# Token mixer: the add of the two partial products of the data moves from GpSimd to VectorE

## The chip, the cores and the metric

One Trainium2 chip, one core. The metric is the device time of the whole program in microseconds, the median of several runs. The cores' engines are named TensorE (PE in the profile), VectorE (DVE), ScalarE (ACT), GpSimd (POOL) and SyncE (SP), which here issues the DMAs.

## The reference

The model makes 64 sequences of 128 image rows and 77 text rows, each of 1024 values, and passes them through a selective scan and a quantized dense layer. Only the first part, the token mixer, is touched. For each of the 128 heads h it builds a kernel from 64 complex modes n and applies it to 64 channels of data c:

```
Wc = W * (exp(dtLambda) - 1) * reciprocal((exp(dtLambda * L) - 1) * Lambda)   # complex, W is the input x
P  = dtLambda[..., None] * pos - P_max[..., None]
K  = einsum('chn,hnl->chl', Wc, exp(P)).real                                   # 64 x 128 x 1024
h  = concatenate([K, txt], axis=1)                                             # then scan, dense layer
```

All of it is f32. The data x is complex, so the product of the data with the complex factor of each mode is a sum of two real products: that sum is the add which the change moves.

## The kernel before, in words

`build` runs its parts one behind the other: `constants`, `token_mixer`, `dense_weights`, `scan_pass` and a general path that is normally empty. The end of a part is a point at which all engines meet. `token_mixer` has 16 steps (G = 0 to 15) of 8 heads each. The first four steps are written out, the other twelve run in a hardware loop of two steps a turn. Partitions hold 64 modes, real parts in the first 64 and imaginary parts in the last 64. The 1024 positions of a head are split: the table (`mag`) has 256 positions, and the data (`gw`) is multiplied with four shifted factors (NQ = 4), so that one matmul of `gw` with `mag` gives all four quarters.

In a step G the engines do this, each in its own order; semaphores tie them:

- VectorE (lines 397 to 422): the angles of 8 heads (line 401, eight instructions, reading one SBUF tensor), their rounding (405) and the subtraction (407), which raises `reduced`. Then, from PSUM, the data times the real factor into `gw` (two instructions of four heads) and times the imaginary factor into `cross` (two more, both line 416, the latter raise `crossed`). Then `evacuate(G - 1)`: the copies of PSUM bank 3 to SBUF (line 395) for heads 3 and 7 of the step before.
- ScalarE (284 to 295): eight Exps for the magnitudes into `mag` (288), the Sin of the angles into `osc` (293) after `reduced`, then the copies of banks 0 to 2 of the step before (282): heads 0, 1, 2, then 4, 5, 6.
- GpSimd (301 to 313): for each side of four heads `mag` times `osc` (line 309, raises `table`), and `gw` plus `cross` (line 312, raises `scaled`).
- TensorE (`step`, lines 443 to 460): head 0 of the step before, the 64 small transposes of this step's data into PSUM (455, raises `x_turned`), and then heads 1 to 7 of the step before (438). A head needs `scaled`, `table` and an empty bank: four banks serve eight heads, so head 4 waits until bank 0 has been copied out, and head 7 until bank 3 has been.
- SyncE: the data of the step after next (line 245, `load`) and the store of the 2 MB of results (252, `store`), two transfers each.

`gw`, `mag`, `res` and the loaded data have two buffers, taken in turns by steps; `cross`, `ang`, `near` and `osc` have one. Nothing else plans the order: it is as written in these step functions.

Of the kernel before, what the change touches and what calls it, by code (L numbers as in the profile page):

```python
# [16 lines left out]
ALU = mybir.AluOpType  # L17
# [22 lines left out]
HG = 8  # L40
# [8 lines left out]
def wait(engine, sem, value):  # L49

    if isinstance(value, int) and value <= 0:
        return
    engine.wait_ge(sem, value)
# [115 lines left out]
def token_mixer(nc, t, dram, mixed):  # L169
# [5 lines left out]
    with ExitStack() as ctx:  # L175
# [24 lines left out]
        cross = sb("t_cross", [P, HG, NQ, BATCH])  # L200
        gw = sb("t_gw", [P, 2, HG, NQ, BATCH])
# [11 lines left out]
        x_turned, crossed, scaled = sem("t_x_turned"), sem("t_crossed"), sem("t_scaled")  # L213
# [7 lines left out]
        def loop(engine, step, tail=None):  # L221

            for G in range(4):
                step(G, G % 2, G == 0)
            with engine.Fori(2, NG // 2) as i:
                step(i * 2, 0, False)
                step(i * 2 + 1, 1, False)
            if tail:
                tail(NG - 1, (NG - 1) % 2)
# [5 lines left out]
        @block.sync  # L235
        def _(sp):
            sp.dma_start(ldt[:, :], dram["log_dt"].rearrange("h r -> (h r)").unsqueeze(0).broadcast_to([P, 2 * HEADS])).then_inc(loaded, 16)
            for k in range(2):
                sp.dma_start(lam[64 * k:64 * k + 64, :], dram["Lambda"]).then_inc(loaded, 16)

            def load(G, half):

                wait(sp, x_turned, G - 1)
                for side in range(2):
                    sp.dma_start(xg[64 * side:64 * side + 64, half, :].rearrange("c (h m) -> c h m", h=HG // 2),
                                 x[:, bass.ds(G * HG + HG // 2 * side, HG // 2), :]).then_inc(x_in[half], 16)

            def store(G, half):
                for b in range(4):
                    wait(sp, empty[b], 2 * G + 2)  # L250
                for a in range(2):
                    sp.dma_start(mixed[:, bass.ds(G * HG, HG), :].rearrange("c h (b a l) -> a c h b l", b=2, a=2)[a],
                                 res[64 * a:64 * a + 64, half, :, :, :]).then_inc(out_done[half], 16)

            load(0, 0)
            load(1, 1)
            with sp.Fori(1, NG // 2) as i:
                load(i * 2, 0)
                store(i * 2 - 2, 0)
                load(i * 2 + 1, 1)  # L260
                store(i * 2 - 1, 1)
            store(NG - 2, 0)
            store(NG - 1, 1)
            for half in range(2):
                sp.wait_ge(out_done[half], 32 * (NG // 2))
# [33 lines left out]
        @block.gpsimd  # L299
        def _(pool):  # L300
            def step(G, half, first):

                for side in range(2):
                    s = slice(side * HG // 2 * QL, (side + 1) * HG // 2 * QL)
                    heads = slice(side * HG // 2, (side + 1) * HG // 2)
                    if side == 0:
                        pool.wait_ge(sine_done, G + 1)
                        pool.wait_ge(mag_done, G + 1)
                    nc.gpsimd.tensor_tensor(mag[:, half, s], mag[:, half, s], osc[:, s], ALU.mult).then_inc(table, 1)  # L309
                    flat = lambda z: z.rearrange("p h a c -> p (h a c)")  # L310
                    pool.wait_ge(crossed, 2 * G + side + 1)
                    nc.gpsimd.tensor_tensor(flat(gw[:, half, heads, :, :]), flat(gw[:, half, heads, :, :]), flat(cross[:, heads, :, :]),
                                            ALU.add).then_inc(scaled, 1)
            loop(pool, step)

        @block.vector
        def _(dve):
            n = [0]
            L = lambda ins: link(dve, dve_step, n, ins)
            V = nc.vector  # L320
# [67 lines left out]
            def evacuate(G, half):  # L388

                wait(dve, out_done[half], out_count(G, half))  # L390
                for h in range(HG):
                    b = h % 4
                    if b in DVE_BANKS:
                        dve.wait_ge(full[b], 2 * G + h // 4 + 1)
                        V.tensor_copy(res[:, half, h, :, :].rearrange("p b l -> p (b l)"), kb[b][:, :]).then_inc(empty[b], 1)

            def step(G, half, first):

                wait(dve, sine_done, G)
                for h in range(HG):  # L400
                    last = V.tensor_scalar(ang[:, h * QL:(h + 1) * QL], pos[:, :], turns[:, bass.ds(G * HG + h, 1)],
                                           role[:, 1:2], ALU.mult, ALU.add)
                last.then_inc(turned, 1)
                dve.wait_ge(turned, G + 1)
                V.tensor_scalar(near[:, :], ang[:, :], ROUND, ROUND, ALU.add, ALU.subtract).then_inc(rounded, 1)
                dve.wait_ge(rounded, G + 1)
                V.tensor_tensor(ang[:, :], ang[:, :], near[:, :], ALU.subtract).then_inc(reduced, 1)

                dve.wait_ge(x_turned, G + 1)
                wait(dve, full[3], 2 * (G - 1))  # L410
                wait(dve, scaled, 2 * G)
                for order, g, target in ((0, gre, gw[:, half, :, :, :]), (1, gim, cross[:, :, :, :])):
                    for side in range(2):
                        heads = slice(HG // 2 * side, HG // 2 * side + HG // 2)
                        data = turned_x[:, side, 256 * order:256 * order + 256].rearrange("p (h c) -> p h c", c=BATCH)
                        last = V.tensor_tensor(
                            target[:, heads, :, :], data.unsqueeze(2).broadcast_to([P, HG // 2, NQ, BATCH]),
                            g[:, bass.ds(G * HG + HG // 2 * side, HG // 2), :].unsqueeze(3).broadcast_to([P, HG // 2, NQ, BATCH]), ALU.mult)
                        if order == 1:
                            last.then_inc(crossed, 1)  # L420
                if not first:
                    evacuate(G - 1, 1 - half)

            loop(dve, step, evacuate)

        @block.tensor
# [1112 lines left out]
```

## Time and profile before

| | us |
|---|---|
| median of 3 runs | 6348.16 |
| lowest and highest | 6346.99, 6351.74 |
| the profiled execution, its own time | 6355.26 |
| its span, first to last instruction | 6353.5 |
| token mixer steps 4 to 14 in it | 188.85 |
| everything after the token mixer | 6008.83 |

The span is what the profile's offsets count from. "Busy" is time in which the engine executes; an interval in brackets at the end of a timeline row is the idle time before it and what ended it. Instructions on one engine may overlap a little at their ends. TensorE's granted clock is given as a share of its full speed: 1.00 is 2.4 GHz and 0.50 is 1.2 GHz.

### The profile page before, as it was taken

The numbers are of one execution on the slowest core, as the hardware profiler recorded it, in microseconds if no ns is written. First come the engines' busy times: TensorE is split into PE (matmuls) and PEld (weight loads), VectorE is DVE, ScalarE is ACT, GpSimd is POOL, SyncE is SP. The second block draws the span as 40 slices with busy tenths as digits, with TensorE's granted clock in tenths as the row PEclk, the third lists the DMA queues.
The fourth block names the chain that finished last, engine by engine and source line by source line (L and its number), as shares of the span: only waits on it lengthen the run. The fifth ranks groups of instructions, "written<-read, shape, count | busy, mean of one in ns | idle before, by whom it ended". The sixth has DMA issues, their size and how long they took to land. (4 is left out here: it accounts for less than half of the span.)

```text
span 6353.5 us, 110648 instructions
## 1 busy us (share of the span) xinstructions
PE 5868.1 (92%) x34115; PEld 5413.4 (85%) x34131; DVE 5699.0 (90%) x4609; ACT 5187.5 (82%) x13015; POOL 5718.5 (90%) x3724
## 2 busy tenths in 40 slices
PE   4667899999999999999999999999999999999998
PEld 3433799999999999999999999999899999999997
DVE  7833999999999999999999999999999999999996
ACT  4646788888888888888888888888888888888885
POOL 3501999999999999999999999999999999999995
PEclk8788999999999999999999999999999999999999
DMA  3510122122211222122221222212222122212220
GB/s 80 139 34 32 70 86 76 62 78 86 86 71 64 81 86 81 65 76 81 86 81 60 79 83 86 76 64 77 86 86 70 65 81 86 81 60 79 83 81 33
DMA packets 113795, 478.62 MB, mean 75 GB/s; under 512 B 13345, under 2 KB 50353, under 8 KB 105074
## 3 DMA queue, kind: packets, MB, share of 16 engines
q1 hardware_dynamic: 113266, 471.63, 21.4%
q8 instruction: 325, 5.32, 0.4%
q14 instruction: 204, 1.67, 0.1%
HBM read 328.35 MB, written 143.24 MB: 74 GB/s over the span
## 5 line engine op out<-in xcount | busy, mean ns | idle before, releaser
L1083 POOL TENSOR_TENSOR s_ring<-s_bc,s_u_t 128x820 f32<-128x820 f32 x2048 | 3626.2, 1790 | 3.5 <-DMA s_bc<-rows_bc 3.5
L989 ACT ACTIVATE s_decay<-s_dt_t,a_neg 128x205 f32<-128x205 f32 x8192 | 3047.2, 420 | 428.4 <-DVE s_ring L1154 360.6
L886 PE MATMUL s_y_ps<-s_ring,ident 128*128 128x205 f32 x16384 | 3166.0, 343 | 138.6 <-POOL s_ring L1089 69.0
L886 PEld LDWEIGHTS s_y_ps<-s_ring,ident 128*128 128x128 f32 x16384 | 2888.5, 193 | 227.1 <-POOL s_ring L1089 133.6
L1148 DVE TENSOR_TENSOR_SCAN s_decay<-s_decay,s_ring 128x820 f32<-128x820 f32 x1216 | 2265.4, 1863 | 221.9 <-ACT s_decay L989 219.3
L1089 POOL TENSOR_TENSOR s_ring<-s_ring,s_bc 128x820 f32<-128x820 f32 x832 | 1607.5, 1932 | 52.1 <-DVE s_ring L1148 52.0
L1148 DVE TENSOR_TENSOR_SCAN s_ring<-s_decay,s_ring 128x820 f32<-128x820 f32 x832 | 1543.6, 1855 | 45.2 <-ACT s_decay L989 44.6
L919 PE MATMUL s_xch<-s_x_t,w_low 128*128 128x205 f32 x8192 | 1522.5, 338 | 0.6 <-ACT s_x_t L1029 0.2
L919 PEld LDWEIGHTS s_xch<-s_x_t,w_low 128*128 128x128 f32 x8192 | 1424.1, 190 | 32.8 <-issue 30.5
L1154 DVE TENSOR_TENSOR s_ring<-s_decay,s_bc 128x820 f32<-128x820 f32 x1216 | 1230.1, 1012 | 41.8
L1029 ACT ACTIVATE s_x_t<-s_xch 128x512 f32<-128x512 f32 (+1 forms) x512 | 245.8, 505 | 92.8 <-PE s_xch L910 90.9
L880 PE MATMUL s_y_ps<-s_x_t,s_d_diag 128*128 128x205 f32 x1024 | 278.6, 354 | 34.9 <-ACT s_x_t L1024 34.9
L1024 ACT ACTIVATE s_x_t<-s_y_ps 128x205 f32<-128x205 f32 x512 | 171.1, 334 | 168.1 <-PE s_y_ps L886 167.3
L1043 ACT ACTIVATE s_y_t<-s_xch,y_bias 128x205 f32<-128x205 f32 x512 | 214.2, 418 | 104.4 <-PE s_xch L919 104.4
L1104 POOL TENSOR_TENSOR s_u_t<-s_dt_t,s_x_t 128x410 f32<-128x410 f32 x256 | 272.3, 1064 | 18.5 <-DVE s_dt_t L1176 18.5
L438 PE MATMUL t_kb<-t_mag,t_gw 128*128 128x256 f32 x512 | 154.7, 469 | 135.7 <-ACT t_res L282 99.3
L438 PEld LDWEIGHTS t_kb<-t_mag,t_gw 128*128 128x128 f32 x512 | 120.4, 241 | 164.5 <-issue 141.4
L951 PE MATMUL s_p_ps<-s_xp,dtw_t 33*128 33x205 f32 x1024 | 247.4, 362 | 7.6 <-DVE s_dt_t L1176 7.1
L880 PEld LDWEIGHTS s_y_ps<-s_x_t,s_d_diag 128*128 128x128 f32 x1024 | 169.2, 189 | 75.4 <-ACT s_x_t L1024 57.2
L309 POOL TENSOR_TENSOR t_mag<-t_mag,t_osc 128x1024 f32<-128x1024 f32 x32 | 75.4, 2355 | 173.6 <-ACT t_osc L293 173.6
L1127 POOL MEMSET s_large<- 128x4 f32 x1 | 0.1, 102 | 247.5 <-POOLq L496 247.5
L951 PEld LDWEIGHTS s_p_ps<-s_xp,dtw_t 33*128 33x128 f32 x1024 | 165.7, 187 | 66.3 <-issue 56.7
(161 smaller groups left out, 4608.9 us busy)
## 6 DMA issues: line engine op xcount, KB each, us to landing
s_bc<-rows_bc SPq DMA_DIRECT2D x64, 3280.0 KB, 11.2
mixed<-t_res SPq DMA_DIRECT2D x32, 1024.0 KB, 10.3
s_x_in<-mixed SPq DMA_DIRECT2D x64, 512.0 KB
s_h<-mixed SPq DMA_DIRECT2D x64, 512.0 KB
before<-s_h SPq DMA_DIRECT2D x64, 512.0 KB
out<-s_h SPq DMA_DIRECT2D x64, 512.0 KB
s_x_in<-in_txt SPq DMA_DIRECT2D x64, 308.0 KB
s_h<-in_txt SPq DMA_DIRECT2D x64, 308.0 KB
```

The lines of the kernel that those rows point to most:

```text
L438: last = nc.tensor.matmul(kb[b][:, QL * k:QL * k + QL], gw[:, half, h, 2 * k:2 * k + 2, :], mag[:, half, h * QL:(h + 1) * QL], start=True, ...
L880: nc.tensor.matmul(y_ps, d_diag[:, j, :], x_t[:, par, j, :], start=True, stop=False)
L886: last = nc.tensor.matmul(y_ps, ident[:, :], ring[:, c % RING, n * LEN:(n + 1) * LEN], start=False, stop=(c % 4 == 3 and n == CN - 1))
L919: last = nc.tensor.matmul(bank[:, 0:LEN], t["w_low"][:, i, P * o:P * o + P], x2_t[:, i, :], start=(i == 0), stop=(i == ND - 1))
L951: last = nc.tensor.matmul(p_ps[:, LEN * k:LEN * k + LEN], t["dtw_t"][:, P * j:P * j + P], xp[0:RANK + 1, :], start=True, stop=True)
L989: last = A.activation(decay[s % 2][:, n * LEN:(n + 1) * LEN], dt_t[:, par, j, :], ACT.Exp, scale=t["a_neg"][:, j, n0 + n:n0 + n + 1])
L1029: A.activation(target[:, 4 * side:4 * side + 4, cols(k)], bank[:, 0:4 * w].rearrange("p (j l) -> p j l", j=4), ACT.Copy).then_inc(empty, 1)
L1083: nc.gpsimd.tensor_tensor(ring[:, s % RING, :].rearrange("p (n l) -> p n l", n=CN), bc[:, par, n0:n0 + CN, :], u_t[:, j, :].unsqueeze(1).b ...
L1089: nc.gpsimd.tensor_tensor(ring[:, c % RING, :], ring[:, c % RING, :], bc[:, par, n0:n0 + CN, :].rearrange("p n l -> p (n l)"), ALU.mult).t ...
L1104: nc.gpsimd.tensor_tensor(u_t[:, 2 * r:2 * r + 2, :], dt_t[:, par, 2 * r:2 * r + 2, :], x_t[:, par, 2 * r:2 * r + 2, :], ALU.mult).then_in ...
L1148: V.tensor_tensor_scan(out=decay[s % 2] if s in ON_DVE else ring[:, s % RING, :], data0=decay[s % 2], data1=ring[:, s % RING, :], initial= ...
L1154: V.tensor_tensor(ring[:, s % RING, :], decay[s % 2], bc[:, par, n0:n0 + CN, :].rearrange("p n l -> p (n l)"), ALU.mult).then_inc(dve_hc, 1)
```

## The change

GpSimd no longer adds: its step holds only the two multiplies of line 309, and their waits. VectorE does the two adds of four heads each, behind its four products and ahead of its copies of bank 3. Each add waits for `crossed` of its side, a semaphore that VectorE itself raised, and raises `scaled` as before. VectorE's own wait on `scaled` before it overwrites `cross` is gone, since the same engine now reads it earlier in its order. TensorE's waits are unchanged.

```diff
--- before.py
+++ after.py
@@ -302,15 +302,10 @@
 
                 for side in range(2):
                     s = slice(side * HG // 2 * QL, (side + 1) * HG // 2 * QL)
-                    heads = slice(side * HG // 2, (side + 1) * HG // 2)
                     if side == 0:
                         pool.wait_ge(sine_done, G + 1)
                         pool.wait_ge(mag_done, G + 1)
                     nc.gpsimd.tensor_tensor(mag[:, half, s], mag[:, half, s], osc[:, s], ALU.mult).then_inc(table, 1)
-                    flat = lambda z: z.rearrange("p h a c -> p (h a c)")
-                    pool.wait_ge(crossed, 2 * G + side + 1)
-                    nc.gpsimd.tensor_tensor(flat(gw[:, half, heads, :, :]), flat(gw[:, half, heads, :, :]), flat(cross[:, heads, :, :]),
-                                            ALU.add).then_inc(scaled, 1)
             loop(pool, step)
 
         @block.vector
@@ -408,7 +403,6 @@
 
                 dve.wait_ge(x_turned, G + 1)
                 wait(dve, full[3], 2 * (G - 1))
-                wait(dve, scaled, 2 * G)
                 for order, g, target in ((0, gre, gw[:, half, :, :, :]), (1, gim, cross[:, :, :, :])):
                     for side in range(2):
                         heads = slice(HG // 2 * side, HG // 2 * side + HG // 2)
@@ -418,6 +412,12 @@
                             g[:, bass.ds(G * HG + HG // 2 * side, HG // 2), :].unsqueeze(3).broadcast_to([P, HG // 2, NQ, BATCH]), ALU.mult)
                         if order == 1:
                             last.then_inc(crossed, 1)
+                flat = lambda z: z.rearrange("p h a c -> p (h a c)")
+                for side in range(2):
+                    heads = slice(HG // 2 * side, HG // 2 * side + HG // 2)
+                    dve.wait_ge(crossed, 2 * G + side + 1)
+                    V.tensor_tensor(flat(gw[:, half, heads, :, :]), flat(gw[:, half, heads, :, :]), flat(cross[:, heads, :, :]),
+                                    ALU.add).then_inc(scaled, 1)
                 if not first:
                     evacuate(G - 1, 1 - half)
 
```

## Rows read from the trace of the kernel before

**Rows 1.** The page: busy time of each engine, share of the span, and count.

```profile
PE 5868.1 (92%) x34115; PEld 5413.4 (85%) x34131; DVE 5699.0 (90%) x4609; ACT 5187.5 (82%) x13015; POOL 5718.5 (90%) x3724
```

**Rows 2.** Table by stage: start:end, length, busy per engine, granted clock, DMA share, GB/s.

```profile
117.02:305.87 188.85, 117.88 (x1057) 94.33 (x1056) 150.34 (x177) 121.33 (x188) 101.26 (x44) 0.80 0.58 138
...
344.67:6353.50 6008.83, 5691.74 (x32562) 5272.59 (x32578) 5449.87 (x4280) 5005.08 (x12737) 5567.73 (x3649) 0.98 0.20 73
```

**Rows 3.** Timeline of step 14: start, us, engine, line, operation, out<-in, count, idle before.

```profile
288.80 4.72 DVE L401 TENSOR_SCALAR t_ang<-t_pos,t_turns,t_role 128x256 f32<-128x256 f32 x8
...
288.99 2.45 POOL L312 TENSOR_TENSOR t_gw<-t_gw,t_cross 128x1024 f32<-128x1024 f32 x1
...
290.07 2.86 PE L438 MATMUL t_kb<-t_mag,t_gw 128*128 128x256 f32 x12
...
294.82 2.29 DVE L407 TENSOR_TENSOR t_ang<-t_ang,t_near 128x2048 f32<-128x2048 f32 x1
297.03 2.35 DVE L416 TENSOR_TENSOR t_gw<-t_turned_x,t_gre 128x1024 f32<-128x1024 f32 x2
297.14 1.91 ACT L293 ACTIVATE t_osc<-t_ang 128x2048 f32<-128x2048 f32 x1 [2.98 <-DVE t_ang L407]
298.96 1.55 ACT L282 ACTIVATE t_res<-t_kb 128x512 f32<-128x512 f32 x3
299.13 2.35 POOL L309 TENSOR_TENSOR t_mag<-t_mag,t_osc 128x1024 f32<-128x1024 f32 x1 [7.70 <-ACT t_osc L293]
299.29 2.35 DVE L416 TENSOR_TENSOR t_cross<-t_turned_x,t_gim 128x1024 f32<-128x1024 f32 x2
...
299.68 6.40 PE L438 MATMUL t_kb<-t_mag,t_gw 128*128 128x256 f32 x20 [6.76 <-ACT t_res L282]
...
301.56 0.68 DVE L395 COPY t_res<-t_kb 128x512 f32<-128x512 f32 x1
301.76 0.60 ACT L282 ACTIVATE t_res<-t_kb 128x512 f32<-128x512 f32 x1 [1.25 <-PE t_kb L438]
303.47 0.60 ACT L282 ACTIVATE t_res<-t_kb 128x512 f32<-128x512 f32 x1 [1.11 <-PE t_kb L438]
...
304.40 0.60 ACT L282 ACTIVATE t_res<-t_kb 128x512 f32<-128x512 f32 x1 [0.33 <-PE t_kb L438]
305.26 0.69 DVE L395 COPY t_res<-t_kb 128x512 f32<-128x512 f32 x1 [3.02 <-PE t_kb L438]
...
305.87 4.72 DVE L401 TENSOR_SCALAR t_ang<-t_pos,t_turns,t_role 128x256 f32<-128x256 f32 x8
...
306.06 2.44 POOL L312 TENSOR_TENSOR t_gw<-t_gw,t_cross 128x1024 f32<-128x1024 f32 x1
```

**Rows 4.** Timeline of steps 0 to 3: the angles (line 401), one table load.

```profile
45.51 2.67 DVE L401 TENSOR_SCALAR t_ang<-t_pos,t_turns,t_role 128x256 f32<-128x256 f32 x8
...
56.22 8.72 DVE L401 TENSOR_SCALAR t_ang<-t_pos,t_turns,t_role 128x256 f32<-128x256 f32 x8
...
79.60 3.99 DVE L401 TENSOR_SCALAR t_ang<-t_pos,t_turns,t_role 128x256 f32<-128x256 f32 x8
...
87.25 1.28 ACT L293 ACT_TABLE_LOAD   x1 [4.11 <-DVE t_ang L407]
...
97.47 4.77 DVE L401 TENSOR_SCALAR t_ang<-t_pos,t_turns,t_role 128x256 f32<-128x256 f32 x8
```

**Rows 5.** Table by stage, one slice of step 14, with its columns' names.

```profile
core 0: us, PE busy (x) PEld busy (x) DVE busy (x) ACT busy (x) POOL busy (x), PEclk, DMA share, GB/s
297.00:303.00 6.00, 3.32 (x8) 2.72 (x9) 5.24 (x6) 3.97 (x5) 3.87 (x2) 0.50 0.61 152
```

**Rows 6.** One line in the scan pass: durations in ns, minimum, median and maximum.

```profile
L1154 DVE TENSOR_TENSOR s_ring<-s_decay,s_bc x1216: 1010/1012/1015, 619.0 to 6284.6; 128x820 f32<-128x820 f32 x174
```

**Rows 7.** Timeline of the scan pass: that line beside a GpSimd multiply.

```profile
3013.75 1.93 POOL L1089 TENSOR_TENSOR s_ring<-s_ring,s_bc 128x820 f32<-128x820 f32 x1
...
3014.63 1.01 DVE L1154 TENSOR_TENSOR s_ring<-s_decay,s_bc 128x820 f32<-128x820 f32 x1
```

## The prediction

> **What bounds the kernel now.** I read the page's line of engines first: all five are busy for 82 to 92% of the span [rows 1], so an average says nothing about a change that touches the token mixer alone. The second view is the table by stage: the eleven mixer steps 4 to 14 take 188.85 us, and the 6008.83 us after the mixer hold no changed instruction [rows 2]. In the eleven steps VectorE is busy 150.34 us, GpSimd 101.26 us, TensorE 117.88 us: 80, 54 and 62%. No engine is full, so it is a chain that sets the step, and the third view, the timeline of one step, shows it.
>
> A step begins where VectorE starts its eight angle instructions (line 401). Step 14 runs from 288.80 to 305.87, 17.07 us [rows 3]. Alone the eight take 2.67 us; beside GpSimd they take 3.99, 4.77 and 8.72 us [rows 4], and 4.72 in step 14. GpSimd's last add of the step before ends at 288.99 + 2.45 = 291.44, and the angle work ends at 293.52, 2.08 later: about six of its eight instructions (0.33 each) run only once GpSimd is done. From there: rounding and subtraction end at 297.11 (3.59), ScalarE's Sin at 299.05 (1.94), GpSimd starts at 299.13 its two multiplies and two adds, and the last add ends at 308.50 (9.45, the gap included). 2.08 + 3.59 + 1.94 + 9.45 = 17.06: this loop is the step of 17.07. GpSimd's four instructions bound the mixer, though GpSimd is busy only 54%, because line 401 cannot run beside them. VectorE's and TensorE's other work hangs on the same loop with slack.
>
> **What goes.** Two GpSimd adds in each of 16 steps. GpSimd then has two multiplies, which start where Sin ends: offset 299.13 - 288.80 = 10.33 in today's step. In the new step everything from line 405 on is earlier by 4.72 - 2.67 = 2.05, so they start at 8.28 and end 2 x 2.35 later, at 12.98. The next line 401 starts well after that (below), so it pays 2.67 again. The wait on `scaled` that VectorE loses never was the late one.
>
> **What comes.** Two VectorE adds of 128x1024, both inputs in SBUF. The nearest rows are line 416, same size, one input in PSUM: the two pairs start 2.26 apart, 1.13 each [rows 3]; and line 407, both inputs in SBUF, 2048 elements in 2.29, half of which is 1.15. Bounds for the pair are 2.2 and, if each keeps its own whole duration with nothing overlapped, 2.45. I take 2.27, since the waits on `crossed` are already met when the adds come up (the first half was counted 1.1 us earlier). Behind the adds on VectorE stands the copy of bank 3 (line 395), and for that TensorE's head 7 waits.
>
> **The new step, offsets from its start.** Line 401 ends at 2.67. Line 407 ends at 297.11 - 288.80 - 2.05 = 6.26. Line 416's last ends at 299.29 + 2.35 - 288.80 - 2.05 = 10.79; the overlap of 0.08 seen between neighbours puts the adds at 10.71 to 12.98. Then comes the copy of bank 3, 0.68, to 13.66. TensorE starts about 0.12 after an emptied bank (298.96 + 0.60 to 299.68), so head 7 starts at 13.78. A head started at 299.68 was followed by its copy at 301.76: 2.08, with a pitch of 303.47 - 301.76 = 1.71 at 1.2 GHz; the pitch at 2.4 GHz is 305.26 - 304.40 = 0.86, so start to copy is 0.86 + 0.37 = 1.23 there. At full clock the second copy starts at 15.01, and the next step 0.61 behind it (305.87 - 305.26): 15.62.
>
> Is head 7 at full clock? Head 4 starts when ScalarE has emptied bank 0, at 299.68 - 288.80 - 2.05 = 8.83. TensorE's earlier work ends at 4.13 (290.07 + 2.86 is 4.13 after 288.80), so it idles 4.7 us instead of 6.8. In step 14 the granted clock was 0.50 from 297 to 303 [rows 5], so it had fallen within 4.1 us of TensorE's stop at 292.93, and it came back not before 3.3 us of new work; head 6's copy follows head 5's by 0.93, almost the fast pitch, so not much later than that. With a similar answer head 7 begins between 13.78 and 13.96 (8.83 + 3 x 1.71, three slow heads), just as the clock is back or somewhat before. That makes 15.6 to 16.1 for the step; I take 15.8.
>
> ScalarE does not come in between: in front of Sin it waited for line 407 (2.98 us in step 14), which comes only 2.05 earlier, so its table and Exps still fit [rows 3]. The transfers move with a share of 0.58 of 17.17 us, 10 us a step [rows 2], below 15.8.
>
> **The sum.** Steps 4 to 14: 188.85 - 11 x 15.8 = 15.1. Step 0 to 1: today line 401 of step 1 starts at 56.22 and ends at 64.94; it will start 2.27 later, at 58.49, and last 2.67: 61.16, saving 3.8. Steps 2 and 3: line 401 goes from 3.99 and 4.77 to 2.67, 1.3 + 2.1 = 3.4 [rows 4]; there ScalarE loads the Sin table, 1.28, only after its wait (the loop's steps load it ahead), so all of TensorE's later heads are 1.3 us later, head 7 is not held by the copy, and the whole saving passes. Step 15: as one more steady step, 17.17 - 15.8 = 1.4; behind it the two last stores (10 us each, one behind the other) follow the same shift. 15.1 + 3.8 + 3.4 + 1.4 = 23.7. The profiled execution ran 6355.26 (span 6353.5); 23.7 less is 6331.6. The median of the runs shown is 6348.16, 7.1 below the profiled one, so the prediction is 6348.16 - 23.7 = 6324.5. A measurement tells no more than about 0.2%, 12.7 us, from no change; the threshold for faster is 6335.5.
>
> **A rule that speaks against it.** In the scan pass VectorE's line 1154 reads two SBUF tensors, as the new adds do. All 1216 of them last 1010 to 1015 ns [rows 6]. The one at 3014.63 lies wholly inside a GpSimd multiply from 3013.75 to 3015.68 that reads two SBUF tensors itself [rows 7]. So neither waited for the other.
>
> The Trainium skill, SBUF — State Buffer, section Who interferes with whom, says that a VectorE instruction with two SBUF inputs contends with a GpSimd instruction that reads SBUF, and that the loser blocks fully. The row differs from it for this pair of shapes; by the rule the step would be that of the lock rival below. For line 401 (one SBUF input, the two-port mode) the same section's lock agrees with [rows 4].
>
> **Rivals.**
> (a) *The lock.* The adds reach VectorE at 10.71, while the second multiply runs (10.6 to 12.98). If they wait for it they run from 12.98 to 15.25, the copy ends at 15.93, head 7 starts at 16.05, its copy at 17.28, and the step is 17.89: 11 x 17.89 is 7.9 more than today. Steps 2 and 3, with the table's 1.3 in front, take 19.2 each, 1.0 more than the 37.42 of today (79.60 to 117.02); step 15 loses 0.7; of step 0's 3.8 the 2.2 of waiting goes off, leaving 1.6 saved. The total is 8 us slower, 6356; with head 7 slow, 0.85 more in each of eleven steps, 6365. It decides as soon as the pair of adds costs about 1.6 us more than 2.27 in each of fifteen steps; below that something is still gained. Against it: [rows 6, 7].
> (b) *TensorE stays slow.* If heads 4 to 7 all run at 1.2 GHz, head 7's copy starts at 8.83 + 4 x 1.71 + 0.37 = 16.04, the step is 16.65, and the savings are 5.7 + 3.8 + 3.4 + 0.5 = 13.4: 6334.8. For it: the clock returned only after 3.3 us of work or more in [rows 5], and head 7 starts 5.0 after head 4, close to that; a later return in some steps costs part of it.
> (c) *Nothing arrives at the end.* The gain is real in the mixer and lost behind it, since 6008.83 us follow whose time differs between executions by several us: 6348. Nothing in the profile waits for a fixed time, so I find no cause.
> On the good side: if the clock never falls (idle 4.7 us), the step is 15.62 (17.0 in all eleven), step 1 could be bound by 58.49 + 15.6 = 74.1 instead of 79.60 - 3.8 = 75.8 (1.7 more): 27.4, 6320.8.
>
> **Chances.** Forecast 0.74, (b) 0.12, (c) 0.07, (a) 0.05, something unseen 0.02. The range 6314 to 6339 takes in the full-clock case and (b), each widened by the 4 us of the runs' spread. (a) and (c) lie outside. Faster: the forecast and most of (b), 0.84; same: the rest of (b), (c) and half of (a), 0.13; slower 0.03.
>
> **What would show it.** In the new trace the GpSimd line of the mixer holds 32 multiplies and no add; line 401's eight take 2.67 in every step; the two adds take 2.27 as a pair beside the second multiply (4.5 would be the lock); VectorE's wait in front of the second bank-3 copy falls from 3.0 to about 1.3; TensorE waits for the bank-3 copy ahead of head 7, a wait that today's timeline does not have; steps are 15.6 to 16.1 apart; the stage behind the mixer keeps its 6008.8. Steps of 16.6 with a clock share of 0.5 throughout heads 4 to 7 would be (b). A step near 17, or adds over 3 us, makes the prediction wrong.

## The result: slightly slower, by the exclusion of VectorE's adds and GpSimd's multiplies

The changed kernel took 6359.69 us (median of 20 runs, 6353.53 to 6364.02), the kernel before 6350.65 (20 runs, 6346.3 to 6355.37). The ratio is 1.0014, interval 1.0008 to 1.0021: some 9 us slower. I had forecast 6324.5, with a range of 6314 to 6339. A change of 0.14% is less than the 0.2% that I had set as the threshold, so it is "same" in the terms of the forecast, to which I had given 0.13 (and 0.03 to slower). It is clear of the runs' noise all the same, since the interval lies above 1. The profiled execution of the changed kernel took 6361.02 us, its span is 6359.2.

**Where the time went.** Table by stage of the changed kernel: steps 4 to 14, step 15 with the stores, and all that follows (columns as in [rows 2]).

```profile
117.65:313.91 196.26, 128.96 (x1057) 98.25 (x1056) 179.33 (x200) 121.37 (x188) 51.30 (x22) 0.79 0.56 132
313.91:353.62 39.71, 19.90 (x127) 15.61 (x125) 17.76 (x21) 14.07 (x23) 4.67 (x2) 0.76 0.67 158
353.62:6359.20 6005.58, 5691.16 (x32578) 5269.17 (x32578) 5448.73 (x4280) 5005.72 (x12737) 5567.71 (x3649) 0.98 0.20 73
```

The eleven steps took 196.26 us instead of 188.85 ([rows 2]), 7.4 more: 17.84 a step, not 15.8. Step 4 begins at 117.65, 0.6 later than before, and step 15 with the stores gives 0.9 more (39.71 against 344.67 - 305.87 = 38.80). The next part starts 8.95 us later; what follows it took 3.25 us less in this one execution. GpSimd's busy time fell from 101.26 to 51.30 us, VectorE's rose from 150.34 to 179.33. Line 401 took 48.49 us in these steps before and takes 29.34 now, 19.1 less. VectorE's busy time rose by 29.0 all the same, so the 22 adds account for 29.0 + 19.1 = 48.1, which is 2.2 each and not the forecast's 1.13. Their own busy time in the trace is 49.0.

**One step.** Timeline of the changed kernel's step 14; line 401 is now 396, 407 is 402, 416 is 410, 395 is 390, 309 is 308, and the new adds are line 419 ([rows 3] answers).

```profile
296.32 2.67 DVE L396 TENSOR_SCALAR t_ang<-t_pos,t_turns,t_role 128x256 f32<-128x256 f32 x8
...
300.28 2.29 DVE L402 TENSOR_TENSOR t_ang<-t_ang,t_near 128x2048 f32<-128x2048 f32 x1
...
304.59 4.67 POOL L308 TENSOR_TENSOR t_mag<-t_mag,t_osc 128x1024 f32<-128x1024 f32 x2 [12.92 <-ACT t_osc L293]
304.75 2.34 DVE L410 TENSOR_TENSOR t_cross<-t_turned_x,t_gim 128x1024 f32<-128x1024 f32 x2
...
305.15 5.10 PE L438 MATMUL t_kb<-t_mag,t_gw 128*128 128x256 f32 x12 [4.71 <-ACT t_res L282]
307.02 4.46 DVE L419 TENSOR_TENSOR t_gw<-t_gw,t_cross 128x1024 f32<-128x1024 f32 x2
...
311.40 0.68 DVE L390 COPY t_res<-t_kb 128x512 f32<-128x512 f32 x1
...
312.13 2.80 PE L438 MATMUL t_kb<-t_mag,t_gw 128*128 128x256 f32 x8 [1.88 <-DVE t_res L390]
313.30 0.69 DVE L390 COPY t_res<-t_kb 128x512 f32<-128x512 f32 x1 [1.22 <-PE t_kb L438]
```

Up to 307.02 the forecast holds to 0.1 us. Line 396 takes 2.67; line 402 ends at offset 6.25 (forecast 6.26); GpSimd starts at 8.27 (8.28); head 4 at 8.83 (8.83); the adds come up at 10.70 (10.71). Then the pair takes 4.46 instead of 2.27. GpSimd's second multiply runs from 306.9 to 304.59 + 4.67 = 309.26, the adds end at 311.48, which is 2.22 after it: neither add executed while the multiply did. The wait is not shown as idle time in front of line 419. It lies inside the duration of the first add (3.32 us; the second takes 1.21), and in the busy share. Everything behind pays: the copy of bank 3 at 311.40, head 7 from 312.13 (TensorE idle for 1.88 us, "DVE t_res L390"), the second copy at 313.30, and the next step at 313.91, 17.59 long.

The lines of the two instructions over the whole trace (columns as in [rows 6]):

```profile
L419 DVE TENSOR_TENSOR t_gw<-t_gw,t_cross x32: 1209/2830/3365, 56.1 to 327.9; 128x1024 f32<-128x1024 f32 x32
```

```profile
L308 POOL TENSOR_TENSOR t_mag<-t_mag,t_osc x32: 2346/2357/3332, 53.7 to 324.5; 128x1024 f32<-128x1024 f32 x32
```

The three figures are minimum, median and maximum. An add takes 1209 ns at best. The median of 2830 is the duration of no add: it lies between two groups. In step 0 and in steps 4 to 15 the first add of a step takes 3.31 to 3.33 us and the second 1.21; in steps 1 to 3 they take 2.35 and 3.36. The products of line 410 (416 before) on the same shape, with one input in PSUM, take 1.2 in the same steps. GpSimd's multiply is 2346 at best and 3332 at most, so it is blocked as well. That happens in steps 1 to 3, where Sin ends late and the first add arrives during the first multiply. Timeline of step 1:

```profile
70.14 5.64 POOL L308 TENSOR_TENSOR t_mag<-t_mag,t_osc 128x1024 f32<-128x1024 f32 x2 [11.75 <-ACT t_osc L293]
...
71.22 5.64 DVE L419 TENSOR_TENSOR t_gw<-t_gw,t_cross 128x1024 f32<-128x1024 f32 x2
```

Both pairs last 5.64. The order that fits is multiply, add, multiply, add, each waiting for the one in flight: 2.35 + about 1 + 2.35 + 1.1, counted from the first multiply to the end of the last add (76.86 - 70.14 = 6.72). In step 14 the adds arrived 0.1 us after the second multiply had begun and waited for that one alone.

Four of the eleven steps were 18.0 to 18.5 long, the other seven 17.6 or 17.65. In the four, the granted clock from head 7's start to its copy was 0.69, 0.50, 0.68 and 0.50; in step 14 it was 0.94. Before that TensorE had stood idle behind the blocked adds, 2.57 us in step 8, which follows, and 1.88 in step 14. Timeline, then the table by stage of that head:

```profile
203.57 0.68 DVE L390 COPY t_res<-t_kb 128x512 f32<-128x512 f32 x1
...
204.30 3.49 PE L438 MATMUL t_kb<-t_mag,t_gw 128*128 128x256 f32 x8 [2.57 <-DVE t_res L390]
206.41 0.69 DVE L390 COPY t_res<-t_kb 128x512 f32<-128x512 f32 x1 [2.17 <-PE t_kb L438]
```

```profile
204.30:206.30 2.00, 2.00 (x5) 1.64 (x6) 0.00 (x0) 0.00 (x0) 0.00 (x0) 0.50 0.00 0
```

Head 7's start to its copy is 206.41 - 204.30 = 2.11, where it is 313.30 - 312.13 = 1.17 in step 14: 0.94 more in step 8, where the granted clock is 1.2 GHz at that place. That is the 0.95 by which step 8 (18.54) is longer than step 14.

### The profile page after: what moved, and what is told of

It reads as the page before. It is cut to its first block and busy times, and to the rows that moved or that the text cites. A ratio compares the mean times of both kernels' runs of the same rounds, so it can differ in the third digit from the quotient of the medians.

```text
span 6359.2 us, 110645 instructions
## 1 busy us (share of the span) xinstructions
PE 5882.3 (92%) x34131; PEld 5415.0 (85%) x34131; DVE 5740.7 (90%) x4641; ACT 5188.2 (82%) x13015; POOL 5647.1 (89%) x3692
## 5 line engine op out<-in xcount | busy, mean ns | idle before, releaser
L919 PEld LDWEIGHTS s_xch<-s_x_t,w_low 128*128 128x128 f32 x8192 | 1427.9, 190 | 33.3 <-issue 30.5
```

What stands on the lines that cost most here:

```text
L919: last = nc.tensor.matmul(bank[:, 0:LEN], t["w_low"][:, i, P * o:P * o + P], x2_t[:, i, :], start=(i == 0), stop=(i == ND - 1))
```

## The experiments

The theory after the result: a VectorE instruction with two SBUF inputs and a GpSimd instruction that reads SBUF exclude each other, and in this order the blocked adds hold up head 7's bank. Rivals: the adds are slow for what they are; VectorE's total time sets the step wherever they stand; any GpSimd work excludes them. The steps below are means over steps 4 to 14, from the starts of the angle instructions in each trace. The medians are of 20 runs for the changed kernel and of 4 to 7 for each experiment, against 9 to 20 of the kernel before on the same chip. Each experiment is an edit of the changed kernel.

| kernel | median us | before, same chip | ratio, interval | step |
|---|---|---|---|---|
| before | | 6350.65 | | 17.17 |
| changed | 6359.69 | 6350.65 | 1.0014, 1.0008 to 1.0021 | 17.84 |
| e1_psum_cross | 6329.19 | 6349.69 | 0.9970, 0.9958 to 0.9981 | 15.88 |
| e2_copy_first | 6323.76 | 6349.69 | 0.9966, 0.9952 to 0.9979 | 15.78 |
| e3_no_mult | 6320.52 | 6349.69 | 0.9956, 0.9941 to 0.9971 | 15.57 |
| e4_no_adds | 6320.60 | 6349.69 | 0.9955, 0.9939 to 0.9970 | 15.29 |
| e5_memset | 6322.51 | 6350.68 | 0.9955, 0.9940 to 0.9971 | 15.66 |
| e6_psum_copy_first | 6320.22 | 6350.68 | 0.9953, 0.9939 to 0.9967 | 15.29 |

**e1_psum_cross: the imaginary product in PSUM.**

```diff
-        cross = sb("t_cross", [P, HG, NQ, BATCH])
+        cross_ps = ctx.enter_context(nc.psum_tensor("t_cross_ps", [P, HG // 2 * NQ * BATCH], F32))
...
+                product(0, 0)
+                product(1, 0).then_inc(crossed, 1)
+                product(0, 1)
+                add(0)
+                dve.wait_ge(scaled, 2 * G + 1)
+                product(1, 1).then_inc(crossed, 1)
...
+                add(1)
```

> The imaginary product of the data goes to PSUM (two banks, used by one side after the other) instead of SBUF, so that each VectorE add has one SBUF and one PSUM input; VectorE's order in a step is real 0, imaginary 0, real 1, add 0, imaginary 1, add 1, and one more wait on its own semaphore stands between. GpSimd's multiplies are unchanged. Theory (a VectorE add with two SBUF inputs and a GpSimd multiply that reads SBUF exclude each other): each add takes 1.2 to 1.35 us beside the second multiply, the step falls from 17.6 to 15.7-16.1 us, total 22 to 26 us below the kernel before, about 6327 where the kernel before is 6350.6. Rival (the adds are slow for what they are, in place and 1024 long, and would be so with GpSimd idle or with PSUM): the pair stays near 4.5 us, step 17.6, total 6360.

Timeline of one step:

```profile
244.03 4.67 POOL L308 TENSOR_TENSOR t_mag<-t_mag,t_osc 128x1024 f32<-128x1024 f32 x2 [11.16 <-ACT t_osc L293]
...
245.32 1.21 DVE L419 TENSOR_TENSOR t_gw<-t_gw,t_cross_ps 128x1024 f32<-128x1024 f32 x1
246.65 1.23 DVE L411 TENSOR_TENSOR t_cross_ps<-t_turned_x,t_gim 128x1024 f32<-128x1024 f32 x1
...
247.92 1.22 DVE L419 TENSOR_TENSOR t_gw<-t_gw,t_cross_ps 128x1024 f32<-128x1024 f32 x1
...
249.06 0.68 DVE L390 COPY t_res<-t_kb 128x512 f32<-128x512 f32 x1
...
251.21 0.69 DVE L390 COPY t_res<-t_kb 128x512 f32<-128x512 f32 x1 [1.47 <-PE t_kb L445]
```

and the adds of the whole mixer:

```profile
L419 DVE TENSOR_TENSOR t_gw<-t_gw,t_cross_ps x32: 1210/1216/1223, 55.2 to 295.6; 128x1024 f32<-128x1024 f32 x32
```

GpSimd's pair of multiplies runs from 244.03 to 248.70. The first add (245.32 to 246.53) lies wholly inside it, the second (247.92 to 249.14) for most of its length, and all 32 take 1210 to 1223 ns. Their order differs a little from the changed kernel's, but both still meet the multiplies; what differs is the memory of one input. That the order alone does not free them is shown by e2, which moves the adds and leaves both inputs in SBUF. So the excess came from the second input's being in SBUF. The steps are 15.8 to 16.1 long, 15.88 in the mean, as expected. The kernel is 0.30% faster than the one before, by 20.5 us, a little less than the 22 to 26 expected.

**e2_copy_first: the adds behind the first copy of bank 3.**

```diff
+                def adds():
+                    for side in range(2):
...
+                if first:
+                    adds()
+                else:
+                    evacuate(G - 1, 1 - half, adds)
```

`evacuate` runs `adds` after the copy of head 3.

> The changed kernel, with the two adds behind the first copy of bank 3 (head 3) instead of ahead of it; both inputs stay in SBUF. Theory (exclusion, and the price is paid because head 7's bank stands behind the blocked adds): the add pair still takes over 4 us of VectorE's time or ends when the second multiply ends plus 2.2, but TensorE no longer waits for the copy of bank 3; adds end at offset 15.2, head 7 is ready at 15.2 to 15.5, step 15.9-16.1, total 6328 to 6334 with the kernel before at 6350.6. Rival (VectorE's total time in a step sets it, wherever the adds stand): step 17.6, total 6360.

Timeline of one step:

```profile
245.91 4.67 POOL L308 TENSOR_TENSOR t_mag<-t_mag,t_osc 128x1024 f32<-128x1024 f32 x2 [11.01 <-ACT t_osc L293]
...
248.33 0.68 DVE L390 COPY t_res<-t_kb 128x512 f32<-128x512 f32 x1
...
248.93 3.86 DVE L423 TENSOR_TENSOR t_gw<-t_gw,t_cross 128x1024 f32<-128x1024 f32 x2
...
252.72 0.68 DVE L390 COPY t_res<-t_kb 128x512 f32<-128x512 f32 x1
```

The exclusion is still there: the pair takes 3.86, and ends at 252.79, 2.21 after the multiplies (245.91 + 4.67 = 250.58). But bank 3 was emptied at 249.01, ahead of it, and head 7 was ready when the adds ended: line 390 follows at once, with no wait. The step is 15.68 here and 15.78 in the mean, 2.1 below the changed kernel's mean. Step and total (6323.76) came out below the 15.9 to 16.1 and 6328 to 6334 expected. The rival that VectorE's total sets the step fails. The price was not the blocked 2.2 us as such, but head 7 standing behind them.

**e3_no_mult and e5_memset: what of GpSimd's work excludes.** In e3 a multiply of one element stands for each table multiply; in e5, behind one such multiply, GpSimd writes 128x2048 zeros twice, into a tile of its own. Both leave the oscillation out of the table.

```diff
-                    nc.gpsimd.tensor_tensor(mag[:, half, s], mag[:, half, s], osc[:, s], ALU.mult).then_inc(table, 1)
+                    nc.gpsimd.tensor_tensor(scratch[:, side:side + 1], t["ident"][:, 0:1], t["ident"][:, 1:2], ALU.mult).then_inc(table, 1)
```

```diff
+                    if side == 0:
+                        nc.gpsimd.tensor_tensor(scratch[:, 0:1], t["ident"][:, 0:1], t["ident"][:, 1:2], ALU.mult)
+                    nc.gpsimd.memset(filler[:, side, :], 0.0).then_inc(table, 1)
```

> The changed kernel without GpSimd's two table multiplies (a 1-element multiply holds the semaphore), so the output of the mixer lacks the oscillation. Theory (exclusion): with GpSimd idle each add takes 1.13 to 1.22 us and the pair 2.3; the step is 15.6-16.1, total 6324 to 6331. Rival (adds slow by themselves): pair 4.5, step 17.6, total 6360.

> The changed kernel with GpSimd's two multiplies replaced by two memsets of 128x2048 into a tile of their own: GpSimd is busy at the same place but reads nothing from SBUF (the mixer's output lacks the oscillation). If what excludes the adds is GpSimd's reading, the adds take 1.13 to 1.22 us each even beside a memset, the step is 15.5 and the total that of the kernel without multiplies, 6320. If any GpSimd instruction excludes them, an add that meets a memset lasts until its end plus 1.1, and the step is longer by what is left of the memset, up to 2 us, total up to 6350.

The adds of e3 in the whole mixer, with both inputs in SBUF:

```profile
L420 DVE TENSOR_TENSOR t_gw<-t_gw,t_cross x32: 1215/1217/1220, 56.2 to 291.9; 128x1024 f32<-128x1024 f32 x32
```

The memsets and the adds of e5, one step and then the whole mixer:

```profile
240.88 3.55 POOL L312 MEMSET t_filler<- 128x2048 f32 x2
...
243.17 2.35 DVE L423 TENSOR_TENSOR t_gw<-t_gw,t_cross 128x1024 f32<-128x1024 f32 x2
```

```profile
L423 DVE TENSOR_TENSOR t_gw<-t_gw,t_cross x32: 1215/1218/1222, 56.3 to 290.8; 128x1024 f32<-128x1024 f32 x32
```

With GpSimd idle the same two-SBUF adds take 1.22 us, so they are not slow by themselves. In e5 GpSimd writes from 240.88 to 244.43 and the adds are up from 243.17: the first lies wholly inside the second memset, as it does in every step, and it takes 1.22 us as well. So GpSimd's activity alone does not exclude them; the instruction that does so reads SBUF. A memset also differs from a multiply in kind, and no experiment varies the kind alone; that the reading is what matters fits these runs, but they do not single it out. The total of e3 came out below the 6324 to 6331 expected, and that of e5 at 6322.51 for 6320.

**e4_no_adds: how much VectorE's own time weighs.** The two adds are left out, so the imaginary part of the data is missing. TensorE then waits for the products:

```diff
-                        pe.wait_ge(scaled, 2 * G + h // 4 + 1)
+                        pe.wait_ge(crossed, 2 * G + h // 4 + 1)
```

> The changed kernel without the two adds (TensorE waits for the products instead), so the imaginary part of the data is left out. Theory (the mixer's next limit is head 7 behind TensorE's slow clock, not VectorE's time): step 15.2-15.9, total 6322 to 6330, within 4 us of the kernel without GpSimd's multiplies. Rival (each us of VectorE counts fully): step 2.2 to 4.4 below the step with adds, 13.2 to 13.6 us, total below 6300.

It came out at 6320.60, equal to e3 with all the adds, and 1.4 below the range expected. VectorE waits for head 7 for 2.8 or 3.9 us in each step there:

```profile
215.16 0.69 DVE L390 COPY t_res<-t_kb 128x512 f32<-128x512 f32 x1 [2.80 <-PE t_kb L432]
...
231.08 0.69 DVE L390 COPY t_res<-t_kb 128x512 f32<-128x512 f32 x1 [3.93 <-PE t_kb L432]
```

Its step is 0.28 us shorter than e3's in these traces (15.29 against 15.57), for some 2.3 us less of VectorE's time. So that time counts for a small part at most, and the rival that asked for a step of 13.2 to 13.6 fails. The run also repeated the other exclusion once: line 396 of step 1 took 4.66 us beside the multiplies that remained.

**e6_psum_copy_first: both remedies.** As e1, with the copy of bank 3 between the first add and the second imaginary product.

> Both remedies together: the imaginary product goes to PSUM, and the first copy of bank 3 stands between add 0 and the second imaginary product. Without exclusion and with head 7 released early (copy done at offset 11.5), TensorE's four heads from offset 8.8 set the end: step 15.0 to 15.9, total 6317 to 6326, like the kernel without adds (6320). If the early copy alone already gives all there is (the adds hidden in the shadow of TensorE), it is within 4 us of the kernel with the copy first (6323.8); if PSUM saves what the blocked adds still cost there, it is lower.

The table by stage of two neighbouring steps, and TensorE's heads from 4 on in each:

```profile
216.14:232.06 15.92, 11.22 (x98) 8.93 (x96) 14.29 (x20) 11.03 (x18) 4.66 (x2) 0.79 0.62 148
232.06:246.86 14.80, 10.09 (x97) 8.15 (x96) 14.29 (x20) 11.03 (x18) 4.67 (x2) 0.88 0.67 159
```

```profile
224.97 7.30 PE L451 MATMUL t_kb<-t_mag,t_gw 128*128 128x256 f32 x20 [4.70 <-ACT t_res L282]
...
240.89 6.18 PE L451 MATMUL t_kb<-t_mag,t_gw 128*128 128x256 f32 x20 [4.71 <-ACT t_res L282]
```

This is as fast as the kernel without the adds, and the fastest here that computes everything: 0.47% below the kernel before. By the medians it is not told apart from e2 (their intervals overlap); in the traces its step is 0.49 us shorter in the mean. Its steps alternate between 15.9 and 14.8 us. In both TensorE is idle for 4.7 us; the step is short where the granted clock is 0.88 on average and the heads take 6.18 in place of 7.30 us.

## Why the prediction was wrong

- **What bounds the kernel before: right.** Without GpSimd's adds line 401 takes 2.67 us in every step, in the changed kernel and in all six experiments but for one place, and where nothing new stood in the way the step fell to 15.3 to 15.9. The loop through GpSimd was the bound.
- **"What comes", the pair of adds at 2.27 us: this step failed.** It was 4.46, and 5.64 in three steps: the sum held a time for two adds that run freely, and nothing for their wait behind the multiply. The bounds I gave, 2.2 and 2.45, did not hold it. The failure came from the section on the rule, where I wrote of line 1154 that it "reads two SBUF tensors, as the new adds do". It doesn't. The kernel declares one of its inputs in PSUM (line 730):

```
decay = [ctx.enter_context(nc.psum_tensor(f"s_decay{i}", [P, 1024], F32))[:, EDGE:EDGE + CW] for i in range(2)]
```

  A row of the trace names tiles, not the memory they are in, and I read the name `s_decay` as an SBUF tile. So [rows 6, 7] show what e1 shows, that a VectorE instruction with one PSUM input runs beside GpSimd at full speed, and were no evidence on the case at hand. Nor were the nearest rows, 416 (one input in PSUM) and 407 (two in SBUF, but GpSimd idle beside it). With the true bound the range would have reached to rival (a). The Trainium skill, SBUF — State Buffer, section Who interferes with whom, says that a VectorE instruction with two SBUF inputs contends with a GpSimd instruction that reads SBUF, and not with one that only writes it. That is rival (a), and the runs agree: adds of up to 3.37 us beside the multiplies, 1.22 beside the memsets (e5).
- **Rival (a) at 0.05 was what happened**, nearly in its numbers: adds ending at 15.16 of the step (forecast 15.25), head 7 at 15.81 (16.05), step 17.59 with head 7 fast (17.89), line 401 of step 1 done at 63.18 and not 64.94, a gain of 1.8 (1.6). The total was 6356 to 6365; 6350.65 x 1.0014 is 6359.7. Its addition of 0.85 for a slow head 7 was seen in four steps of eleven, as 0.95 in two and 0.4 in two. What it lacked is that the multiplies are blocked too: with pairs of 5.64 in steps 1 to 3, step 4 began 0.6 later than before, where the rival had it 0.6 earlier (1.6 saved, 1.0 lost).
- **The sum apart from that: right.** e1, which does what I thought the change did, has a step of 15.88 (forecast 15.8, range 15.6 to 16.1), and is 20.5 us below the kernel before (forecast 23.7). In its trace steps 4 to 14 take 174.66 us, a saving of 14.2 (forecast 15.1), and steps 0 to 3 take 63.19 in place of 71.51, a saving of 8.3 (forecast 3.8 + 3.4 = 7.2).
- **The low-clock rival (b)** asked for heads at 1.2 GHz through the step's end. With the exclusion gone (e1) no step was over 16.1. In the e1 step shown, the granted clock was 0.50 from 244.58 to 249.06 and 0.81 over head 7 (1.42 us from its start to its copy, where the forecast had 1.23 at full clock and 2.08 at 1.2 GHz), so head 7 was mostly back at full clock, as forecast; in e4 and e6 every second step shows the difference, 1.1 us.
- **Rival (c), a gain that is lost behind the mixer: refuted by the experiments.** In the traces the last copy of bank 3 ends 23.4 us earlier than in the kernel before in e1, 23.0 in e2, 26.8 in e3, 29.9 in e4, 28.6 in e5 and 29.5 in e6; the medians are 20.5, 25.9, 29.2, 29.1, 28.2 and 30.5 lower. What the mixer gains arrives at the end, to within some 3 us.
- **The wait on `scaled`, the transfers, ScalarE's place:** as forecast, no wait on them stands in the rows above.

## What to carry to other kernels

Before moving work from GpSimd to VectorE, look up for both the memory of every input, in the declarations and not by the tile's name: here a VectorE add with two SBUF inputs did not run beside a GpSimd multiply that reads SBUF, while one with an input in PSUM did. If the collision can't be avoided, put whatever another engine waits for ahead of the instruction that will be blocked; here that order alone turned 0.14% slower into 0.34% faster. A blocked instruction shows as a long one, not as a wait, so compare each duration in a trace with the shortest of the same shape.

## What the runs showed of the hardware that I had not expected

The exclusion works both ways and by single instructions: in steps 1 to 3 multiplies of 2.35 us and adds of 1.2 us took turns, and both pairs lasted 5.64 us. A GpSimd memset beside the same adds cost neither anything: the 32 memsets of e5 take 1.80 to 1.81 us each, beside an add or not. A VectorE add of SBUF and PSUM takes the same 1.22 us as one of two SBUF tensors with GpSimd idle (e1 and e3), so for this size the PSUM input is free.
